# A GNN, attention and expert kernel on one core: the selection matrix of a run made by ScalarE in two operations

## The reference

```python
z = h @ W_func.T
concat_z = jnp.concatenate([z[edge_src], z[edge_dst], w], axis=-1)
e = jax.nn.leaky_relu(concat_z @ W_att.T, negative_slope=NEG_SLOPE)[:, 0]
m = jax.ops.segment_max(e, edge_dst, num_segments=N)
e_exp = jnp.exp(e - m[edge_dst])
denom = jax.ops.segment_sum(e_exp, edge_dst, num_segments=N)
agg = jax.ops.segment_sum((e_exp / denom[edge_dst])[:, None] * z[edge_src], edge_dst, num_segments=N)
```

## Time and profile before

| what | value |
|---|---|
| median of 3 executions | 2236.36 us |
| the profiled execution | 2231.19 us |
| its span, first to last instruction | 2229.4 us |
| step loop, groups 1 to 23 | 366.8 to 1627.3 us of the span |
| PE busy in the span | 1856.3 us (83%) |
| POOL busy | 1400.0 us (63%) |
| DVE busy | 1445.7 us (65%) |
| ACT busy | 1068.8 us (48%) |
| mean granted TensorE clock | 0.885 of full speed |

### The profile page before, as it was taken

One profiled execution on the slowest core, in us unless ns is written; L12 is line 12 of the kernel. 1 busy time (PEld: TensorE's weight loads), 2 busy tenths in 40 slices (PEclk: granted clock), 3 DMA queues, 4 the chain that ended last, 5 costly groups with the idle time before them and its releaser, 6 DMA issues.

```text
span 2229.4 us, 36374 instructions
## 1 busy us (share of the span) xinstructions
PE 1856.3 (83%) x9283; PEld 1391.0 (62%) x9283; DVE 1445.7 (65%) x3688; ACT 1068.8 (48%) x3294; POOL 1400.0 (63%) x1102
## 2 busy tenths in 40 slices
PE   6899449888898888898888888888887788899991
PEld 4555336656666666666665666666654478788981
DVE  6989337666676766666666666666666756345574
ACT  2444335545554555555555555555554344455550
POOL 5000688888888888888888888888700435734266
PEclk9999768889888998888898988888888889999996
DMA  8999364555555555555555555555429634545464
GB/s 198 291 276 277 86 155 118 144 141 151 150 160 133 147 159 142 144 151 146 144 142 145 142 141 144 149 149 146 120 66 241 176 105 137 152 132 150 137 176 123
DMA packets 312783, 344.97 MB, mean 155 GB/s; under 512 B 127407, under 2 KB 270490, under 8 KB 309455
## 3 DMA queue, kind: packets, MB, share of 16 engines
q1 hardware_dynamic: 169765, 198.42, 31.6%
q0 software_dynamic: 135840, 137.77, 24.9%
q10 hardware_dynamic: 6975, 6.45, 1.0%
HBM read 254.64 MB, written 86.69 MB: 153 GB/s over the span
## 4 chain that ended last, share of the span: by engine, by line
PE 47%; POOL 13%; DMA 12%; DVE 11%; issue 11%; SPq 2%; DVEq 1%; another core or an unknown queue 1%; ACT 1%; ACTq 0%; POOLq 0%
PE bank L710 44%; POOL wexp L663 11%; DMA wexp<-func_rows,a_src 9%; DVE acc L1879 3%; SPq L406 2%; DMA g_all<-sorted_d 1%; DVE wexp L1464 1%; POOL g_all L697 1%; DVEq L1879 1%; PE bank L1047 1%; PE bank L858 1%; DVE work L1638 1%; DMA work<-in_wv 1%; DVE acc L1467 1%
## 5 line engine op out<-in xcount | busy, mean ns | idle before, releaser
L663 POOL DMA_INDIRECT wexp<-func_rows,a_src x850 | 1107.5, 1303 | 436.3 <-issue 205.6
L710 PE MATMUL bank<-wexp,onehot 125*125 125x257 f32 x1700 | 616.8, 468 | 81.4 <-DVE acc L1879 63.5
L1879 DVE SCALAR_TENSOR_TENSOR acc<-acc,corr,bank 125x257 f32 x850 | 400.4, 471 | 313.5 <-PE bank L710 176.5
L1201 ACT ACTIVATE onehot<-iota_r,a_rel 125x125 f32<-125x125 f32 x850 | 335.1, 394 | 441.3 <-PE bank L710 345.7
L710 PEld LDWEIGHTS bank<-wexp,onehot 125*125 125x125 f32 x1700 | 332.8, 220 | 239.8 <-issue 108.6
L1209 ACT ACTIVATE onehot<-onehot,a_p 125x125 f32<-125x125 f32 x850 | 327.8, 386 | 3.4 <-issue 3.4
L687 POOL DMA_INDIRECT sorted_d<-acc,work x100 | 121.1, 1211 | 220.3 <-DVE acc L2014 140.5
L710 PE MATMUL bank<-g_all,wexp 128*128 128x128 f32 x1840 | 230.1, 277 | 12.2 <-issue 7.1
L710 PEld LDWEIGHTS bank<-g_all,wexp 128*128 128x128 f32 x1840 | 217.2, 193 | 17.0 <-issue 10.6
L697 POOL DMA_INDIRECT g_all<-y_d,work x100 | 130.6, 1306 | 139.1 <-DVE g_all L2184 75.3
L710 PE MATMUL bank<-work,w_s 128*128 128x250 f32 x800 | 211.2, 387 | 2.0
(11 more groups left out here) (271 smaller groups left out, 2655.8 us busy)
## 6 DMA issues: line engine op xcount, KB each, us to landing
rel_oh<-rel_d SPq DMA_DIRECT2D x50, 531.2 KB
wexp<-in_attr SPq DMA_DIRECT2D x25, 896.0 KB
sorted_d<-spare SPq DMA_DIRECT2D x72, 256.0 KB
g_all<-sorted_d SPq DMA_DIRECT2D x115, 128.0 KB
y_d<-g_all SPq DMA_DIRECT2D x115, 128.0 KB
wexp<-func_rows,a_src POOLq DMA_INDIRECT x850
work<-xn_rows SPq DMA_DIRECT2D x38, 224.0 KB
xnT_d<-work SPq DMA_DIRECT2D x25, 250.0 KB, 9.2
```

Of the source, the lines that this page charges most:

```text
L663: pool.indirect_dma_start(ring[:, n % RING, :], None, func_rows, bass.IndirectOffsetOnAxis(ap=a_src[:, n // CS, n % CS:n % CS + 1], axis=0 ...
L710: return pe.matmul(o, l, r, start=first, stop=last_, **kw)
L1201: act.activation(onehot[:, n % AHEAD, :], iota_r[:], ACT.Abs, bias=a_rel_v[:, n:n + 1], scale=-1.0).then_inc(s("far"), 1)
L1879: v.scalar_tensor_tensor(to, to, corr[:, k % 2, y:y + 1], bank[3 + n % 2][0:R, 0:D + 1], ALU.mult, ALU.add).then_inc(s("summed"), 1)
```

## The change

The selection matrix is made by ACT. Two activations, in place on `rel_oh`, take the place of DVE's comparison: Abs of (`iota_p` minus the target's number), a distance, and the exponential of -1000 times the distance, which is 1 at distance 0 and 0 elsewhere. Both are on all 128x2128 elements. The second waits for the first, and `look_up` on PE waits for the second through a semaphore of its own, `k_oh`; a second wait there keeps an order on DVE that the old one implied. The place in the order of steps is the same: `one_hot` still comes at the start of the step z=3 or z=20, now in ACT's `select`.

```diff
-BY_DVE = dict(oh=0, u0=3, u1=3, t=6, le=6, sf=7, sb=8, start=11, run=11, min=12, max=12, row=12, mi=15, cm=15, f2=16, p=17, ap=20)
+BY_DVE = dict(u0=3, u1=3, t=6, le=6, sf=7, sb=8, start=11, run=11, min=12, max=12, row=12, mi=15, cm=15, f2=16, p=17, ap=20)
...
             def look_up(k):
 
-                pe.wait_ge(s("k_dve"), scored(k, "oh"))
+                pe.wait_ge(s("k_oh"), 2 * k + 2)
+                freed(pe, s("k_dve"), scored(k - 1, "p"))
                 for z in range(RUN):
...
+            def one_hot(k):
+
+                act.wait_ge(s("rel_in"), 16 * (k + 1))
+                act.activation(rel_oh[:], rel_oh[:], ACT.Abs, bias=iota_p[:], scale=-1.0).then_inc(s("k_oh"), 1)
+                act.wait_ge(s("k_oh"), 2 * k + 1)
+                act.activation(rel_oh[:], rel_oh[:], ACT.Exp, scale=-APART).then_inc(s("k_oh"), 1)
+
             def select(n):
 
                 for k, at in runs_at(n):
+                    if at == 0:
+                        one_hot(k)
                     if at == CORR:
                         rescale(k)
...
-            def one_hot(k):
-
-                v.wait_ge(s("rel_in"), 16 * (k + 1))
-                v.tensor_scalar(rel_oh[:], rel_oh[:], iota_p[:], None, ALU.is_equal).then_inc(s("k_dve"), 1)
-
...
                 for k, at in runs_at(n):
-                    if at == BY_DVE["oh"]:
-                        one_hot(k)
                     if at == BY_DVE["u0"]:
```

## The result

The changed kernel takes **2312.56 us** in the median (2311.3 to 2318.37, 4 executions) against 2241.35 (2234.39 to 2246.82, 4 executions) for the kernel before beside it: a ratio of 1.0324, 95% interval 1.0284 to 1.0365, so 71 us slower. The forecast was 2285 us, 49 us slower, within 2228 to 2335. Direction, the main mechanism and the range held; the size was short by a third, and a good part of it has another source than the forecast gave.

The account below looks back on a forecast made before the run. POOL's gathers were taken to bound the kernel, with the pace passing to PE: -87.5 (gather waits) -11 (their slow clock) +103 +4 (new waits) +41 (new slow clock) = +49 us on 2236.36, so 2285 us, range 2228 to 2335.

Parts of the forecast that it names:

- The bound: Step loop: POOL's back-to-back gathers set the pace at 54.80 us a group; PE waits 3.80 us a group at `turn_scores`.
- The pair: The two new activations on ACT for each run: 4.13 us from start to PE, no table load, bf16 output no dearer.
- The stall at z=5: PE waits at `look_up` in even runs for ACT's activations, 4.46 us later than before, 23 times: 103 us.
- The waits for gathers: PE's waits at `turn_scores` for the run's last gather, 87.5 us in 23 groups, were to vanish.
- The slow clock right after the stall: After each new PE stall at z=5, a stretch of low clock costing 1.8 us, 23 times: 41 us.
- The 11 us of old slow clock: Low clock at z=8 to 22 after gather waits, 1.8 us in 6 of 23 groups, was to go.
- the sum: All terms over the loop: -87.5 -11 +103 +4 +41 = +49 us; a group takes 56.9 instead of 54.80 us.
- The other slow stretch: Low clock at z=25 to 34, about 12 us a group, was to stay whatever happens to the waits: no change.
- The odd pair, z=22: Odd runs' activations, placed at z=20: PE waits 0.17 us at `look_up`, 23 times: 4 us.
- What POOL gets back: Gathers beside the removed comparisons get shorter, freeing about 37 us of POOL, which counts only if POOL sets the pace.
- The 8 us set aside for the neighbours of the comparison: Of 45 us extra in gathers overlapping comparisons, 8 us come from neighbouring operations and would stay.
- The rival "POOL keeps the pace and gets faster": If PE's new stall is under 2.5 us with no slow clock, POOL's freed 37 us come through: 2199 us; chance 0.12.

Follow-up runs that it names:

- experiment 5: Changed kernel with only the odd runs' matrix made on ACT, DVE comparing for even runs: 2210.4 us, 0.9891 of the kernel before.
- experiment 7: Changed kernel with the even runs' pair of activations one step earlier in ACT's list, at z=2: 2174.7 us, 0.9733 of the kernel before.
- experiment 9: Kernel before with one more wait on DVE ahead of the comparison, leaving a gap there: 2208.1 us, ratio 0.9835.
- experiment 10: Kernel before with one more wait on DVE behind the comparison, leaving a gap there: 2225.9 us, ratio 0.9894.
- experiment 11: Kernel before with DVE's comparison in two halves, the second waiting for the first: 2203.9 us, ratio 0.9811.
- experiment 1: Changed kernel with no selection matrix made on either engine, scores wrong: 2198.4 us, 0.9812 of the kernel before.
- experiment 2: Changed kernel with the even runs' pair of activations nine steps earlier in ACT's list: 2204.7 us, 0.9836 of the kernel before.
- experiment 3: Kernel before, DVE's comparison kept, plus two idle activations of the same size on ACT at the pair's place: 2263.6 us, ratio 1.0114.
- Experiment 6: Changed kernel with only the even runs' matrix made on ACT, DVE comparing for odd runs: 2265.8 us, 1.0157 of the kernel before.
- experiment 8: Kernel before with DVE's comparison made a second time, in two halves into a spare tile ahead of the used one: 2191.5 us, ratio 0.9820.

## Why the prediction was right, and where it was short

- **The bound: right.** POOL set the pace, PE's reserve was the wait at `turn_scores`. Experiments 5, 7, 9, 10 and 11 show it from the other side: there the group follows POOL's pace to 0.12 us. It is not so wherever PE has no long stall: in experiments 1 and 2 the group is 0.80 and 0.77 us longer than the pace.
- **The pair: right.** 4.13 us forecast; 2.06 + 1.98 and 0.05 us to PE, with 0.04 us between the two. The price by columns from the earlier trace rows held to 0.01 us for each activation, the bf16 output was not dearer, and no table was loaded.
- **The stall at z=5: right.** 4.46 us forecast, 4.42 measured. What is queued behind the pair on ACT is as late as the pair, so that the stall stands one product later when PE does not wait for the pair itself (experiment 3). What takes it away is another place in ACT's list (experiment 7).
- **The waits for gathers: right.** 87.5 us forecast to go, all gone.
- **The slow clock right after the stall: right.** 1.8 us forecast. z=5 to 8 takes 6.09 us where the groups of before that waited for nothing there took 4.4: 1.7 us. It lay in z=5 to 8, not in z=8 to 22, which had been named as the place to look; by that sign alone the step would have been called wrong. The 11 us of old slow clock that the sum took off in z=8 to 22 came back only in small part: the stage is 0.06 us a group shorter, not 0.48.
- **The other slow stretch: the mis-sized term.** "So it stays whatever happens to the waits" was the step that failed. The stretch of z=25 to 34 did not stay: it begins later and goes on in z=0, which takes PE's full time: z=25 to 34 +0.34 and z=0 to 3 +0.66 us, 23 x 1.00 = 23 us that the sum had at nothing. The forecast's +2.13 us a group becomes the measured +2.86 with these 1.00, 0.14 more at z=3 to 5 (4.60 against 4.46), and some 0.4 less in z=5 to 25, where the sum had -2.3 (the waits, their clock, the new slow clock, z=22) and the table has -2.75.
- **The odd pair, z=22: wrong.** 4 us forecast, for its own wait. Experiment 6 shows 33 us, and no wait for the matrix among it; it is there only beside the even stalls, since alone the odd pair cost nothing (experiment 5). Half a microsecond of the 1.45 lies in the two stages just named (+0.42 and +0.06), the rest in z=3 to 25. The even stalls without it gave 35 us, less than the forecast, so that a part of the forecast's size came right for a reason that it did not have.
- **What POOL gets back: too small, without effect.** 37 us forecast, 59 measured. The 8 us set aside for the neighbours of the comparison were not lost but joined by 15 more: gathers that overlap no comparison were 33 us over the median before and are 18 now. It changed nothing since PE is the bound. The reason given, that the comparison holds a gather for its own time, was incomplete: what counts is whether VectorE has a gap ahead of the comparison (experiments 8, 9 and 11), and, where TENSOR_TENSOR L1638 follows the comparison, one behind it (experiment 10).
- **The rival "POOL keeps the pace and gets faster"** named its own condition, a pair that starts before `m_queries`. Experiment 7 is that case: 0.9733 of the time before, where 2199 of 2236 us (0.983) had been worked out.

## What to carry to other kernels

An operation that is moved to a less busy engine costs what its place in that engine's list costs: look at which instruction stands ahead of it, who waits for it and who for what is queued behind, and find the place where that engine rests; one step in the list was worth some 130 us here (ratio 1.0324 against 0.9733). Before an operation is moved to get it out of another engine's way, find out what of it is in the way: a wait that costs 0.1 us, or the operation in halves, gave two thirds of the best gain. And a stretch at the low clock is no constant: when the waits of PE move, ask where each slow stretch will begin and what PE has to do in it.

## What the runs showed of the hardware

- A gather on POOL (1.21 us alone) is held up by VectorE's comparison of 128x2128 in bf16, by up to 0.99 us (2.20), and to the end of a TENSOR_TENSOR of 125x512 where that follows second behind it without a gap, by up to 1.89 us; a BATCH_NORM_STATS2 in its place does not hold it. A gap of 0.04 to 0.11 us on VectorE ahead of the comparison is enough to let a gather through that starts from 0.1 us ahead of it to 0.03 us behind it (1.21 to 1.22 us); one that starts 0.5 us ahead still takes 1.61 to 1.63 us, or holds the comparison (up to 1.20 us instead of 0.76). A second comparison that brings such gaps makes the kernel 40 us faster.
- An activation of 128x2128 takes 2.06 us with a bias per partition and 1.98 without, in bf16 in place, and as much with uint8 output (2058 and 1977 ns in experiment 3).
- PE's low clock of 1.2 GHz came to 15.2 us a group before, 19.1 after and 10.8 and 11.6 in the kernels 2 and 7, with the same matrix products in each; a stall of 4.4 us was followed each time by 3 to 5 us of it within z=5 to 8.
